# A graph layer on one core: P from a row-scaled triangle of M with 64 products a pair instead of 72, mask products on GpSimd, and another order of a pair's lists

## The reference, cut to what matters

```python
z_l = x @ W_lang.T; z_g = x @ W_grav.T; v = x @ W_V.T      # x: 32 batches of 256 x 512, float32
zn  = z_l / max(norm(z_l), EPS)
A_l = max(zn @ zn.T, 0) * not_eye
d2  = max(sq + sq.T - 2 * z_g @ z_g.T, 0)
A_g = exp(-d2 / (2 * sigma**2)) * not_eye
K_l = A_l * adj / max(rowsum(A_l * adj), EPS)              # K_g from A_g in the same way
K   = w_l * K_l + (1 - w_l) * K_g
out = layernorm(x + (K @ v) @ W_O.T)
```

## Time and profile before

| | us |
|---|---|
| median of 3 runs | 686.14 (685.93 to 686.62) |
| the profiled execution | 686.16 |
| its span in the trace | 684.4 |
| PE busy | 675.4 (99%) |
| DVE busy | 518.0 (76%) |
| ACT busy | 364.7 (53%) |
| POOL busy | 132.4 (19%) |
| one pair (300.00 to 339.90) | PE 39.90, DVE 31.36, ACT 21.81, POOL 7.83 busy |

### The profile page before, as it was taken

The page is one execution under the profiler, slowest core; times in us unless marked ns, Lnnn a source line. Parts: engine busy times, 40 slices in busy tenths (PEclk is TensorE's granted clock), DMA queues, the critical chain, the costliest instruction groups (busy, mean ns, idle before and its releaser), DMA issues.

```text
span 684.4 us, 10995 instructions
## 1 busy us (share of the span) xinstructions
PE 675.4 (99%) x3020; PEld 559.6 (82%) x3020; DVE 518.0 (76%) x1396; ACT 364.7 (53%) x705; POOL 132.4 (19%) x278
## 2 busy tenths in 40 slices
PE   8999999999999999999999999999999999999995
PEld 7888888888888888888888888888888888888884
DVE  4645878788697878869787886978788697877876
ACT  5434445645455564545556454555645455564646
POOL 3302021111222111122211112221111222121122
PEclk9999999999999999999999999999999999999999
DMA  9312726473664647366464636646473664636523
GB/s 291 92 34 67 218 79 191 127 209 112 194 184 141 189 132 197 115 197 181 140 188 131 202 112 196 182 140 188 136 196 112 194 184 141 186 109 184 162 70 123
DMA packets 141510, 106.50 MB, mean 156 GB/s; under 512 B 40112, under 2 KB 115632, under 8 KB 141488
## 3 DMA queue, kind: packets, MB, share of 16 engines
q1 hardware_dynamic: 140768, 104.40, 51.2%
q0 software_dynamic: 288, 1.05, 0.5%
q10 hardware_dynamic: 432, 0.79, 0.3%
HBM read 65.80 MB, written 40.40 MB: 155 GB/s over the span
## 4 chain that ended last, share of the span: by engine, by line
PE 98%; DMA 0%; DVE 0%; issue 0%; ACT 0%; POOL 0%; POOLq 0%
PE bank L1264 95%; PE bank L1286 2%; DMA xs<-in_L_gnn_W_lang 0%; PE bank L1368 0%; PE bank L1296 0%; PE bank L1291 0%; PE bank L1378 0%; DVE xq L1166 0%; DVE p_lo L858 0%; ACT p_hi L617 0%; POOL last_rstd L589 0%; POOLq L53 0%; DVE xq L1186 0%; DVE last_shift L1181 0%; DVE last_rstd L1175 0%
## 5 line engine op out<-in xcount | busy, mean ns | idle before, releaser
L1264 PE MATMUL bank<-hT_lo,m_hi 128*128 128x512 f32 x512 | 168.0, 389 | 0.0
L662 ACT CAST p_hi<-bank 128x512 fp32r<-128x512 f32 x128 | 73.5, 588 | 101.4 <-PE bank L1264 101.4
L1264 PE MATMUL bank<-hT_hi,m_lo 128*128 128x512 f32 x320 | 124.5, 389 | 0.0
L921 DVE TENSOR_TENSOR p_lo<-bank,p_hi 128x512 fp32r<-128x512 f32 x128 | 85.3, 687 | 39.1 <-ACT p_hi L662 37.5
L1264 PEld LDWEIGHTS bank<-hT_lo,m_hi 128*128 128x128 f32 x512 | 96.1, 188 | 20.1 <-DVE p_lo L921 0.2
L662 ACT CAST v_hi<-bank 128x512 fp32r<-128x512 f32 x60 | 32.5, 590 | 132.1 <-PE bank L1264 132.1
L1264 PE MATMUL bank<-wvo_hi,hT_hi 128*128 128x512 f32 x256 | 99.8, 390 | 0.0
L1264 PE MATMUL bank<-wvo_hi,hT_lo 128*128 128x512 f32 x256 | 99.6, 389 | 0.0
L1264 PE MATMUL bank<-wvo_lo,hT_hi 128*128 128x512 f32 x256 | 99.6, 389 | 0.0
L1264 PE MATMUL bank<-p_lo,hT_hi 128*128 128x512 f32 x256 | 99.6, 389 | 0.0
L1264 PE MATMUL bank<-p_hi,hT_hi 128*128 128x512 f32 x256 | 99.6, 389 | 0.0
(11 more groups left out here) (140 smaller groups left out, 1213.4 us busy)
## 6 DMA issues: line engine op xcount, KB each, us to landing
x_blk<-in_x SPq DMA_DIRECT2D x128, 128.0 KB, 3.0
x_spill<-xs SPq DMA_DIRECT2D x30, 512.0 KB, 3.4
xq<-x_spill SPq DMA_DIRECT2D x120, 128.0 KB, 3.1
x_nat<-in_x SPq DMA_DIRECT2D x30, 512.0 KB, 4.7
out_y<-y SPq DMA_DIRECT2D x30, 512.0 KB, 3.0
k_spill<-work SPq DMA_DIRECT2D x30, 256.0 KB, 2.1
work<-k_spill SPq DMA_DIRECT2D x120, 64.0 KB, 2.1
r_row<-r_spill SPq DMA_DIRECT2D x32, 128.0 KB, 3.5
```

The costliest lines, as they stand in the source:

```text
L662: nc.scalar.copy(dst, src).then_inc(proj_hi, 1)
L921: nc.vector.tensor_tensor(dst, src, hi.bitcast(F32), ALU.subtract).then_inc(proj_ready, 1)
L1264: last = pe.matmul(dst, lhsT, rhs, start=(n == 0), stop=(n == len(steps) - 1))
```

## The change

1. **Row-scaled triangle.** M's rows are divided by a factor (`m_scale`, close to 1) that makes the diagonal's lo part vanish, so that the upper triangle's rest, minus its diagonal, can be put into one stationary block with the lower triangle. `md_hi` of a block now holds the lower half of `m_hi` (diagonal halved) plus the strictly upper part of `m_lo`. A projection is then 4 matmuls with hi of x and 4 with lo of x, 8 for every block: 64 a pair. The factor is multiplied back where P is read: ACT's copy becomes an activation with a scale, DVE's subtraction a scalar_tensor_tensor.
2. **In the preparation** DVE takes the diagonals (`diagonals`), makes the factors (`scales`) and rescales `m_lo` (`scaled_rest`); POOL builds two masks and joins the triangles (`join_triangles`). ACT no longer writes `md_hi`. PE's first projections wait for `m_ready`.
3. **Projections** go L first (k = 0..3), then G, and each does its hi products ahead of its lo products.
4. **`inverse_masked`** moves from DVE's lists to POOL's.
5. **Other order** of the pair's lists on SP, ACT and DVE, and in-place reuse of `den`. The lists of the last pair stay, but for the `inverse_masked` that leaves DVE's.

The core of the diff:

```diff
@@ gpsimd
+            def join_triangles(g):
+                pool.wait_ge(m_scaled[g], DT)
...
+                for part, (tile, mask) in enumerate(((m_hi, lower_half), (m_lo, upper_strict))):
+                    many, one = diagonal_blocks(tile, g)
+                    nc.gpsimd.tensor_tensor(triangle(part)[:, 0:DT - 1], many.bitcast(F32),
+                                            mask.unsqueeze(1).broadcast_to([P, DT - 1, P]), ALU.mult).then_inc(m_parts[g], 1)
+                    nc.gpsimd.tensor_tensor(triangle(part)[:, DT - 1], one.bitcast(F32), mask, ALU.mult).then_inc(m_parts[g], 1)
+                pool.wait_ge(m_parts[g], 4)
+                nc.gpsimd.tensor_tensor(md_hi[:, g], triangle(0), triangle(1), ALU.add).then_inc(m_ready[g], 1)
+
+            join_triangles(L)
             pool.wait_ge(adj_loaded, 16)
...
             def pair(p):
                 q = p - 1
+                inverse_masked(q, 0)
                 for b in range(2):
                     mean(q - 1, b)
-                for b in range(2):
-                    layer_norm(q - 1, b)
+                layer_norm(q - 1, 0)
+                inverse_masked(q, 1)
+                layer_norm(q - 1, 1)
@@ scalar
-                    nc.scalar.copy(m_hi[:, g, i, i * P:], src[:, i * P:])
-                    nc.scalar.mul(md_hi[:, g, i], src[:, i * P:(i + 1) * P], 0.5).then_inc(prep_hi, 1)
+                    nc.scalar.copy(m_hi[:, g, i, i * P:], src[:, i * P:]).then_inc(prep_hi, 1)
...
-                    dst = p_hi[:, :, k // 2, k % 2, :]
-                    src = src[:].rearrange("p (b n) -> p b n", b=2)
+                    j, g = of_projection(k)
+                    nc.scalar.activation(p_hi[:, :, j, g, :], src[:].rearrange("p (b n) -> p b n", b=2), ACT.Copy,
+                                         scale=m_scale[:, g, j:j + 1]).then_inc(proj_hi, 1)
@@ vector
+            def diagonals(g, i):
+                dve.wait_ge(prep_lo, prepared(UPPER, g, i))
+                for s, (tile, sign) in enumerate(((m_hi, 1.0), (m_lo, -1.0))):
+                    nc.vector.tensor_tensor_reduce(
+                        out=x_nat[:, g, s, a:e], in0=tile[:, g, i, a:e].bitcast(F32), in1=ident[:], scale=sign, scalar=0.0,
+                        op0=ALU.mult, op1=ALU.add, accum_out=steps_of[g][:, s, i:i + 1]).then_inc(m_scale_steps[g], 1)
...
+            def scaled_rest(g):
+                for i in range(DT):
+                    nc.vector.scalar_tensor_tensor(
+                        out=m_lo[:, g, i, i * P:], in0=m_hi[:, g, i, i * P:].bitcast(F32), scalar=steps_of[g][:, 4, i:i + 1],
+                        in1=m_lo[:, g, i, i * P:].bitcast(F32), op0=ALU.mult, op1=ALU.add).then_inc(m_scaled[g], 1)
...
-                    hi, dst = p_hi[:, :, k // 2, k % 2, :], p_lo[:, :, k // 2, k % 2, :]
-                    src = src[:].rearrange("p (b n) -> p b n", b=2)
+                    j, g = of_projection(k)
+                    nc.vector.scalar_tensor_tensor(
+                        out=p_lo[:, :, j, g, :], in0=src[:].rearrange("p (b n) -> p b n", b=2), scalar=m_scale[:, g, j:j + 1],
+                        in1=p_hi[:, :, j, g, :].bitcast(F32), op0=ALU.mult, op1=ALU.subtract).then_inc(proj_ready, 1)
@@ tensor
+                if type(p) is int and p == 0 and j == 0:
+                    pe.wait_ge(m_ready[g], 1)
+                    pe.wait_ge(prep_lo, prepared(MIRROR, g, DT - 1))
...
-                for i in range(DT):
-                    steps.append((m_hi[:, g, i, c], lo[i]))
-                    if i <= j:
-                        steps.append((m_hi[:, g, i, c] if i < j else md_hi[:, g, i], hi[i]))
-                        steps.append((m_lo[:, g, i, c], hi[i]))
-                products(pbank(k)[:], steps).then_inc(proj_done, 1)
+                for i in range(DT):
+                    stationary = m_lo[:, g, i, c] if i < j else md_hi[:, g, i] if i == j else m_hi[:, g, i, c]
+                    pe.matmul(pbank(k)[:], stationary, hi[i], start=(i == 0), stop=False)
+                if k == 0:
+                    pe.wait_ge(hT_ready, upto(p, 2, 2))
+                for i in range(DT):
+                    last = pe.matmul(pbank(k)[:], m_hi[:, g, i, c], lo[i], start=False, stop=(i == DT - 1))
+                last.then_inc(proj_done, 1)
```

More of the change, by code:

```diff
@@ L32 @@
 EPS = 1e-8
+TINY = 1e-35
 LN_EPS = 1e-5
@@ L126, in gnn_resnorm, with diagonal_blocks, split_blocks, triangle @@
         last_shift = sb("last_shift", [P, 2, NT])
+        lower_half = junk_d[:, 0, 0]
+        upper_strict = junk_d[:, 0, 1]
+        steps_of = [junk_d[:, 1, 1, 32 * g:32 * g + 32].rearrange("p (s j) -> p s j", j=DT) for g in range(2)]
+        def diagonal_blocks(tile, g):
+            flat = tile[:, g].rearrange("p k d -> p (k d)")
+            step = D + P
+            return (flat[:, 0:(DT - 1) * step].rearrange("p (i w) -> p i w", w=step)[:, :, 0:P], flat[:, (DT - 1) * step:])
+        def split_blocks(tile, g):
+            flat = tile[:, g].rearrange("p k c -> p (k c)")
+            return (flat[:, 0:(DT - 1) * P].rearrange("p (i c) -> p i c", c=P), flat[:, (DT - 1) * P:])
+        def triangle(part):
+            return junk_a[:].rearrange("p t (k c) -> p t k c", c=P)[:, part]
         COS, GAUSS, KER = range(3)
@@ L213, in gnn_resnorm @@
         adj_ready = sem("adj_ready")
+        masks_cleared = sem("masks_cleared")
+        masks_ready = sem("masks_ready")
+        m_scale_steps = [sem(f"m_scale_steps{g}") for g in range(2)]
+        m_scaled = [sem(f"m_scaled{g}") for g in range(2)]
+        m_parts = [sem(f"m_parts{g}") for g in range(2)]
+        m_ready = [sem(f"m_ready{g}") for g in range(2)]
         scal_exp = sem("scal_exp")
@@ L891, in _ @@
                     weight_lo(G, 2 + i)
+                if kind == UPPER and g == L:
+                    diagonals(L, i)
+                    if i == DT - 1:
+                        scales(L)
+                        scaled_rest(L)
+                if kind == UPPER and g == G and i < DT - 1:
+                    diagonals(G, i)
                 if u in SPLIT_AT:
@@ L895, in _ @@
                     turn(0, TURN_AT[u])
+                if (kind, g, i) == (MIRROR, G, 1):
+                    diagonals(G, DT - 1)
+                    scales(G)
+                if (kind, g, i) == (WVO, None, 1):
+                    scaled_rest(G)
             turn(1, 0)
@@ L1086, in pair @@
                 turn_lo(p + 1, 1 - parity, 1)
+                turn(p + 2, 0)
+                proj_lo_part(p, 8)
+                proj_lo_part(p, 9)
                 turn_r(p, 1)
[L1088 removed]
+                turn_k(q, 1)
                 residual(q, 0, 0)
+                kt_lo_part(q, 1)
                 residual(q, 0, 1)
[L1091 to L1095 removed]
+                turn_x(p, 0)
                 residual(q, 1, 0)
[L1097 removed]
                 gram(p, 0, G)
                 proj_lo_part(p, 10)
+                residual(q, 1, 1)
                 proj_lo_part(p, 11)
[L1101 removed]
             dve.wait_ge(adj_ready, 1)
             dve.wait_ge(scal_steps, 8)
+            for g in (L, G):
+                dve.wait_ge(m_scale_steps[g], 2 * DT + 4)
+                dve.wait_ge(m_ready[g], 1)
             pair(0, 0)
```

126 lines of the change are left out of this document (70 added, 56 removed).

## The result

The changed kernel takes 666.67 us, median of 4 runs (666.07 to 666.71), the kernel before, on the same chip, 686.03 (685.8 to 686.62). The ratio is 0.9714, 95% interval 0.9698 to 0.9731: 19.4 us less. Forecast were 662 us, range 656.9 to 668.5, and "faster" with 0.96; the narrower range of the forecast's own case, 659.5 to 666.5, is missed by 0.2 us.

What follows compares the result with a forecast made beforehand. PE was taken as the bound, waiting for nobody from 30 to 655 us. The sum was 686.2 - 29.0 (matmuls) + 4.0 (preparation) + 1.0 (last pair) = 662.2, so 662 us, range 656.9 to 668.5.

Steps and rivals of the forecast that it cites:

- the forecast's own case: Whole kernel: 662 us, with its own range 659.5 to 666.5 and a chance of 0.55.
- Matmuls, 29.0: PE's projections: 128 fewer matmuls at 0.2267 us save 29.0 us; a pair takes 38.08 us.
- DVE and ACT in a pair, nothing: Pairs 0 to 14: the changed DVE and ACT instructions and lists make PE wait for nothing.
- Mask products: `inverse_masked` on POOL: 1.29 us each, taken to hold DVE up to 1.29 us per product; nothing in a steady pair.
- 2.7 us of room: DVE ahead of a steady pair's first x tile: 1.6 idle plus 1.1 slack it can lose before PE waits.
- Rival A: No lock on DVE, only POOL suffers: preparation costs 0.3 and last pair 0.5, 658.0 us; chance 0.25.
- B: A wait in every pair: a 3.1 us POOL product makes PE wait 0.4 us in 14 pairs, 668; chance 0.15.
- C: Slower than before: a mask product holding DVE over 4.4 us; at 5.2 us, 697; chance 0.03.
- Preparation, 4.0: DVE's added diagonals, scales and rescalings beside POOL's W_V split delay PE by 4 us, from a range of 0.3 to 7.
- the kinder case: Preparation: DVE keeps the port between rescalings, the last ending near 20.2 and PE's third block 2.0 us late.
- my seven held instructions: Preparation: seven DVE instructions with two SBUF inputs, each waiting 0.6 or 1.3 us if taking turns with POOL.
- Last pair, 1.0: Last pair's unchanged, tighter lists: PE waits 1.0 us for the last lo part, between 0.5 and 1.8 missing.

Runs made afterwards that it cites:

- e5: Changed kernel with the mask products back on DVE and the steady pairs' SP, ACT and DVE lists of the kernel before, leaving the triangle alone: 667.85 us.
- e2: Changed kernel with W_V not split: POOL only fills its two parts with constants by memsets, which write but do not read SBUF: 662.7 us.
- e3: Changed kernel with the mask products given back from POOL to DVE, each right ahead of its cosine mask: 666.89 us.
- e9: Changed kernel, last pair's ACT and DVE lists reordered: projection copies and lo parts earlier, first batch's diagonals ahead of turning the second kernel matrix: 665.21 us.
- e8: Changed kernel with 20 matmuls on zeros ahead of every wait of the preparation's third block, to fill PE's stand: 666.71 us.
- e1: Changed kernel with M_L's scales and rescalings moved behind M_G's first mirror, after POOL's W_V split, and M_G's moved later too: 661.18 us.

## Why the prediction was right, and where it was off

- *Matmuls, 29.0.* Right: 2892, a pair of 38.08 us, nothing lost in pairs 0 to 14. e5 shows that the triangle alone brings them, without the other lists or the move of the mask products.
- *DVE and ACT in a pair, nothing.* Right in sum. I had reckoned with 1.6 us idle and a slack of 1.07 at the first x tile; the rows have 1.53 and 1.05. One price was wrong: the lo part costs 742 ns, not 678 to 687. ACT's copy costs 686 ns, within the bound of 729.
- *Mask products.* Right for POOL: 1309 ns each against 1.29. What they take from DVE was oversized: I took 1.29 us a product; the sums lose 0.46 on average (13.9 us over 30 products) and 0.88 at most (one sum of 1564 ns). With 2.7 us of room it made no difference. Rival A (no lock on DVE) is refuted by 0.69 against 1.31 us and by e2; B and C by the pairs.
- *Preparation, 4.0.* The mechanism was right, the size wrong: 7.5, over my upper end of 7. The first part was in the text, as the end "near 22.7" and "4.5 us late" of the case in which each instruction takes its turn; measured were 22.68 and 4.5. I averaged it with the kinder case. That it fits so closely is partly luck: the TENSOR_SCALAR, held for 1 us, was not among my seven held instructions, POOL began 0.5 us earlier than in rows 7 (13.65), and the rescalings took 4.31 us where I had named 5 or more as the sign; with the same code the third block starts at 22.24 in e3 and at 21.79 in e9, and only the first projection hardly moves (42.72, 43.01). The second part I did not count: TensorE's clock behind a stand of 4.7 us (1.3 us, e8), and DVE's diagonals of M_G ahead of what PE waits for. These I had named, but only as a reason for the upper end; they have 1.53 us of the chain, and no run takes them out, so that they are the other 1.7 us is read from the chain and not tested. A late start is not simply carried on: what stands behind it ran without slack. (A slip that changes nothing: 3.3 us of work in a gap of 2.85 is 0.45 us late, not 0.3.)
- *Last pair, 1.0.* Mis-sized too: 2.1. The wait at the first x tile was 0.6 us, not 1, and a second one, 0.8 us for projection 3's lo part, was not in my sum: I had followed only the last lo part. Giving the mask products back to DVE doesn't help (e3 has 56.4 us there, 0.5 more); the order of the lists is the cause (e9).
- *Sum and range.* 662.2 + 3.5 + 1.1 = 666.8, against 666.67 in the profiled execution. The two terms for the ends were too small by 4.6 us together. The measured time lies beyond my own case (659.5 to 666.5) and within the wide range only because rival B, a wait in every pair, had stretched that to 668.5. B did not happen, so that part of being right is luck.

## What to carry to other kernels

Work that is moved to an idle stretch of DVE must be checked against what GpSimd does in that stretch: here two SBUF inputs on the one and reads on the other took turns instruction by instruction (4.31 us against 1.93), and where two ends of a range differ by "takes turns" or "keeps the port", take the turns. Put such work where GpSimd is idle, even if that is later. And when the pace of a steady loop changes, go through the prologue and the last iteration wait by wait: all 9.6 us that this change gave back lay there, and moving entries of its lists got 7.6 of them again.

## What the runs showed of the hardware that was not expected

- A TENSOR_SCALAR on 128x4 fp32 out of and into SBUF takes 0.15 to 0.17 us alone, 1.21 beside a reading GpSimd instruction and in one row 0.51 beside a GpSimd memset, ending with it both times. A RECIPROCAL of the same size took 0.18 us beside a cast (the changed kernel) and beside a memset (e2).
- The clock fell to 1.2 GHz behind a stand of 4.7 us (granted 0.50; 128x256 products 0.21 instead of 0.12 us apart), but in e2 also after waits of only 0.48 and 0.95 us among small transposes (12 products 4.58 us instead of 3.01), while in e1 one wait of 0.59 at the same place left it up (its clock's line has a 9 in every slice but the last).
- A scalar_tensor_tensor out of PSUM whose scalar comes from a tile takes 742 ns for 512 columns, the tensor_tensor 687 and a scalar_tensor_tensor with a constant 678.
